# Attention queries made a batch ahead as rows of tokens, turned by VectorE and through DRAM

## The reference

```python
lat = layer_norm(latents, ln2_w, ln2_b)
lat = lat * (1.0 + scale[:, None, :]) + shift[:, None, :]
q = jnp.einsum('bld,ed->ble', lat, Wq)
kv_in = jnp.concatenate((x, lat), axis=-2)
kv = jnp.einsum('bld,ed->ble', kv_in, Wkv)
logits = jnp.einsum('bhqd,bhkd->bhqk', q * attn_scale, k * attn_scale)
w = jax.nn.softmax(logits.astype(jnp.float32), axis=-1).astype(logits.dtype)
out = jnp.einsum('bhqk,bhkd->bhqd', w, v)
return jnp.einsum('ble,de->bld', out, Wo)
```

## Time and profile before

| | |
|---|---|
| time, median of 3 runs | 685.08 us (683.45 to 686.34) |
| the profiled execution's own time | 684.31 us |
| its span, first to last instruction | 682.6 us |
| granted TensorE clock, mean | 0.997 |
| busy: TensorE, weight loads | 671.4 us (98%), 625.0 us (92%) |
| busy: VectorE, ScalarE, GpSimd | 470.2 us (69%), 430.6 us (63%), 269.2 us (39%) |
| query products, L1052 | 64.0 us in 512 passes |

### The profile page before, as it was taken

The page is one execution under the profiler, slowest core; times in us unless marked ns, Lnnn a source line. Parts: engine busy times, 40 slices in busy tenths (PEclk is TensorE's granted clock), DMA queues, the critical chain, the costliest instruction groups (busy, mean ns, idle before and its releaser), DMA issues. The chain is left out here.

```text
span 682.6 us, 17910 instructions
## 1 busy us (share of the span) xinstructions
PE 671.4 (98%) x5935; PEld 625.0 (92%) x5936; DVE 470.2 (69%) x970; ACT 430.6 (63%) x1166; POOL 269.2 (39%) x428
## 2 busy tenths in 40 slices
PE   8899999999999999999999999999999999999997
PEld 8789899999998999989989988898899999999997
DVE  7787877877787788787797766366645775444443
ACT  4888878788788888888878855242334554222222
POOL 2853243342433343324547441056520453424333
PEclk9899999999999999999999999999999999999999
DMA  7645455455455444545546434002668999888870
GB/s 279 190 121 149 121 145 146 130 146 146 124 140 150 131 131 138 156 120 139 147 132 171 106 94 132 1 1 96 180 217 244 299 346 294 256 266 258 259 245 5
DMA packets 77935, 111.76 MB, mean 164 GB/s; under 512 B 28732, under 2 KB 45758, under 8 KB 77632
## 3 DMA queue, kind: packets, MB, share of 16 engines
q1 hardware_dynamic: 66016, 92.73, 45.7%
q0 software_dynamic: 8864, 18.38, 9.5%
q10 hardware_dynamic: 3008, 0.03, 0.3%
HBM read 63.74 MB, written 16.67 MB: 118 GB/s over the span
## 5 line engine op out<-in xcount | busy, mean ns | idle before, releaser
L1034 PE MATMUL PS<-BIG 128*128 128x256 f32 (+1 forms) x1164 | 195.8, 322 | 3.1 <-ACT V L635 2.0
L1034 PEld LDWEIGHTS PS<-BIG 128*128 128x128 f32 x1164 | 163.9, 190 | 20.3 <-issue 5.1
L653 ACT ACTIVATE PR<-PS,NMX 128x256 f32<-128x256 f32 x256 | 119.2, 483 | 40.9 <-DVE NMX L838 40.9
L2092 PE MATMUL PS<-XST,W 128*128 128x128 f32 x1012 | 117.0, 275 | 0.3 <-DMA W<-in_w 0.3
L2092 PEld LDWEIGHTS PS<-XST,W 128*128 128x128 f32 x1012 | 115.1, 192 | 0.5 <-DMA W<-in_w 0.5
L496 POOL DMA_DIRECT2D PT<-PR x128 | 65.3, 515 | 125.0 <-DVE PR L850 81.0
L662 ACT ACTIVATE PR<-PR,RINV 128x256 f32<-128x256 f32 x256 | 106.1, 519 | 0.0
L850 DVE STREAM_TRANSPOSE PR<-PR 128x512 f32<-128x512 f32 x124 | 82.2, 691 | 4.6 <-ACT PR L662 1.5
L838 DVE TENSOR_REDUCE NMX<-PS 128x4 f32<-128x1024 f32 x64 | 75.6, 1201 | 0.1
L1587 POOL DMA_INDIRECT out_x<-YS,WHO x23 | 31.7, 1377 | 87.7 <-DVE YS L1954 76.9
L1052 PE MATMUL PS<-KVF,WQ 128*128 128x128 f32 x512 | 64.0, 278 | 0.0
(11 more groups left out here) (187 smaller groups left out, 1101.1 us busy)
## 6 DMA issues: line engine op xcount, KB each, us to landing
PT<-PR SPq DMA_DIRECT2D x368, 64.0 KB, 2.3
W<-in_w SPq DMA_DIRECT2D x29, 640.0 KB, 4.5
W<-in_w SPq DMA_DIRECT2D x21, 768.0 KB
PT<-PR POOLq DMA_DIRECT2D x128, 64.0 KB, 2.5
turned<-CXN SPq DMA_DIRECT2D x15, 256.0 KB, 2.0
INT<-turned POOLq DMA_DIRECT2D x56, 64.0 KB, 2.8
xs_sorted<-C SPq DMA_DIRECT2D x26, 128.5 KB, 3.0
W<-in_w SPq DMA_DIRECT2D x8, 352.0 KB, 3.4
```

Source lines behind the costliest of these rows:

```text
L653: last = act.activation(probs, logits, ACT.Exp, bias=NMX[:, g, own, p % 2:p % 2 + 1], accum_out=SUM[:, p, own:own + 1])
L1034: last = pe.matmul(dst, stat(s, k), mov(m, k), start=n == 0, stop=n == len(todo) - 1)
L2092: last = pe.matmul(h[:, P * c:P * (c + 1)], lhs13(W13[par], k, c), XST[par][:, :, k, :], start=k == 0, stop=k == KD - 1)
```

## The change

The queries of h = 6 to 29 (`TURNED`, batches 3 to 14) are made in another way and earlier.

- TensorE (`q_turned`): six products of 512 columns in the split form, tokens stationary, weights moving, so that bank 4 holds rows of tokens. Both halves of batch b+1 are made in batch b: the first half's behind the keys in the first half of b, the second half's where the next batch's first half stood. The rounded query weights WQS lie in the memory that WS13, the shared expert's weights, takes later; GpSimd splits them in batch 1 (`queries_split`).
- VectorE (`q_turn`) transposes the bank in 32x32 blocks into QT; SyncE (`store_queries`) stores it to DRAM; GpSimd (`load_queries`) loads it in four DMAs with the blocks exchanged, as QF. ScalarE (`q_hi_turned`) and VectorE (`q_lo_turned`, four subtractions of 128x128) make the high and low part from QF.
- Since keys and values of b+1 are now read in the first half of b, the inputs come earlier: from batch 1 on statistics, rows, conditions and input transpose of batch b+2 are in the first half of b and not in the second, and `modulate(b + 2)` is in the second half of b, where before `modulate(b + 1)` was in the first half of b. SyncE loads the rows of b+3 in batch b, GpSimd loads INT of b+2 at the end of batch b. ScalarE's KVH of the next batch goes from the end of the first half's normalisation to the start of the half.
- The descriptor memory of GpSimd's DMAs is halved, to make room for QT and QF.

The diff, cut to its core:

```diff
+            "queries": [dram(f"queries{i}", [P, INNER // 2]) for i in range(2)],
...
+TURNED = (6, 2 * NB - 3)
...
+    views["WQS"] = [w[:, :, :].rearrange("p k f -> p (k f)")[:, 0:KD * INNER].rearrange("p (h k e) -> p h k e", h=2, k=KD)
+                    for w in views["WS13"]]
...
+            def store_queries(h, H):
+                sp.wait_ge(v_qt, nth_turned(h))
+                sp.nop(nofuse=True)
+                sp.dma_start(mem["queries"][H], QT[:, :]).then_inc(d_qs, 16)
...
+            def batch(n, stored=True, rows=True, second=False, last=False, ahead=False):
+                if ahead:
+                    store_queries(2 * n + 2, 0)
+                if stored:
+                    store_inputs(n + 2)
                 if rows:
-                    load_rows(n + 2)
-                if first:
-                    load_inputs(sp, 1)
-                    load_late()
+                    load_rows(n + 3)
                 move_probs(n, 0)
-                if not first:
-                    load_residual(n - 1)
-                    if not second:
-                        store_sum(n - 2)
-                if rows:
-                    store_inputs(n + 2)
+                load_residual(n - 1)
+                if not second:
+                    store_sum(n - 2)
+                if ahead:
+                    store_queries(2 * n + 3, 1)
                 if not last:
...
+            def load_queries(h, H):
+
+                pool.wait_ge(d_qs, 16 * nth_turned(h))
+                pool.nop(nofuse=True)
+                pool.wait_ge(v_q, h)
+                pool.nop(nofuse=True)
+                for i in range(4):
+                    pool.dma_start(QF[QUADS[i], :, :],
+                                   mem["queries"][H][:, 128 * i:128 * (i + 1)].rearrange("(j c) f -> c j f", j=4))\
+                        .then_inc(d_qf, 16)
+
+            def queries_split(H, k):
+
+                parts = [t.rearrange("x (i p c) -> x i p c", i=4, p=HP) for t in (WQS[0][:, H, k, :], WQS[1][:, H, k, :])]
+                raw = WQ[:, H, k, :].rearrange("x (p i c) -> x i p c", i=4, p=HP)
+                pool.tensor_copy(parts[0], raw).then_inc(p_wqh, 1)
+                pool.wait_ge(p_wqh, KD * H + k + 1)
+                pool.tensor_tensor(parts[1], raw, parts[0].bitcast(FP32), ALU.subtract).then_inc(p_wql, 1)
+
+            def batch_1():
+                keep_probs(0, 1)
+                load_inputs(pool, 2)
+                kv_lo(2, 0)
+                norms(3)
+                keep_probs(1, 0)
+                load_inputs(pool, 3)
+                for H in range(2):
+                    for k in range(KD):
+                        queries_split(H, k)
+
+            def batch(b, par, following=True, norm=True, between=None, turned=True, ahead=True):
                 if following:
                     kv_lo(b + 1, 1 - par)
-                if not (isinstance(b, int) and b == 1):
-                    rstd(3, 1, v_mv3, p_ve3, p_rs3, b - 1)
+                if turned:
+                    load_queries(2 * b + 1, 1)
+                keep_probs(b - 1, 1)
+                if norm:
+                    norms(b + 2)
+                early_parts = HP if between else 0
+                for j in range(early_parts):
+                    between(j)
+                rstd(3, 1, v_mv3, p_ve3, p_rs3, b - 1)
+                if ahead:
+                    load_queries(2 * b + 2, 0)
                 keep_probs(b, 0)
                 if norm:
-                    norms(b + 2)
+                    load_inputs(pool, b + 2)
...
+            def q_hi_turned(h, H):
+                act.wait_ge(d_qf, 64 * nth_turned(h))
+                act.nop(nofuse=True)
+                act.wait_ge(t_lg, 2 * (h - 1))
+                act.activation(QH[:, HP * H:HP * (H + 1), :].rearrange("x p (j r) -> x j p r", j=4),
+                               QF[:, :, :].rearrange("x j (p r) -> x j p r", p=HP), ACT.Copy, scale=QSCALE).then_inc(a_q, 1)
...
+            def q_turn(h):
+                dve.wait_ge(t_q, h + 1)
+                if not (isinstance(h, int) and h == TURNED[0]):
+                    dve.nop(nofuse=True)
+                    dve.wait_ge(d_qs, 16 * (nth_turned(h) - 1))
+                dve.transpose(QT[:, :], PS[:, PROJ[0], :]).then_inc(v_qt, 1)
+
+            def q_lo_turned(h, H):
+                dve.wait_ge(a_q, h + 1)
+                for p in range(HP):
+                    low, high = (t[:, HP * H + p, :].rearrange("x (j r) -> x j r", j=4) for t in (QL, QH))
+                    last = dve.scalar_tensor_tensor(low, QF[:, :, 32 * p:32 * (p + 1)], QSCALE, high.bitcast(FP32),
+                                                    ALU.mult, ALU.subtract)
+                last.then_inc(v_q, 1)
...
-            def half_0(b, par, first=False, second=False, last=False):
+            def half_0(b, par, first=False, second=False, norm=True, turned=False, ahead=False):
                 h = 2 * b
                 row_max(h, 0)
-                q_lo(h + 1, 1)
+                if not turned:
+                    q_lo(h + 1, 1)
                 row_max(h, 1)
                 k_lo(h + 1, 1, 0)
                 k_lo(h + 1, 1, 1)
                 inverse_sums(h, 0)
-                if first:
+                if first or second:
                     modulate(b + 1, 1 - par)
+                if norm and not first:
+                    norm_stats(b + 2)
+                if ahead:
+                    q_turn(h + 2)
                 inverse_sums(h, 1)
+                if norm and not first:
+                    norm_rows(b + 2)
+                    conditions(b + 2)
+                    transpose_inputs(b + 2)
                 if not first and not second:
                     residual(b - 2)
-                transpose_blocks(h, 0, 0)
-                if not first and not last:
-                    modulate(b + 1, 1 - par)
-                for p in (1, 2, 3):
+                if turned:
+                    q_lo_turned(h + 1, 1)
+                for p in range(HP):
                     transpose_blocks(h, 0, p)
...
+                if ahead:
+                    q_lo_turned(h + 1, 0)
+                elif not final:
+                    q_lo(h + 1, 0)
                 if not final:
-                    q_lo(h + 1, 0)
                     for p in (0, 1):
                         transpose_blocks(h, 1, p)
                 else:
                     residual(b - 1)
-                if norm:
+                if first:
                     conditions(b + 2)
                     transpose_inputs(b + 2)
+                if norm and not first:
+                    modulate(b + 2, par)
+                if ahead:
+                    q_turn(h + 2)
                 if not final:
                     for p in (2, 3):
                         transpose_blocks(h, 1, p)
...
+            def q_turned(h, b, H, par):
+
+                if H == 0:
+                    pe.wait_ge(p_wql, 2 * KD)
+                    pe.wait_ge(a_kvh, b + 1)
+                    pe.wait_ge(p_kvl, b)
+                    if isinstance(h, int) and h == TURNED[0]:
+                        pe.wait_ge(v_q, h)
+                    else:
+                        pe.wait_ge(v_qt, nth_turned(h) - 1)
+                else:
+                    pe.wait_ge(v_ol, h - 3)
+                kv = (KVH[par], KVL[par])
+                split3(PS[:, PROJ[0], :], lambda s, c: kv[s][:, c, P:KEYS], lambda m, c: WQS[m][:, H, c, :],
+                       range(KD)).then_inc(t_q, 1)
...
+                    if taken is not None:
+                        pe.wait_ge(v_qt, nth_turned(taken))
...
-                if not first:
+                if not first and not turned:
                     q_unit(h + 1, b, 1, par)
                 for i in range(2):
                     k_unit(h + 1, b, 1, par, i)
+                if ahead:
+                    q_turned(h + 2, b + 1, 0, 1 - par)
...
-                    times_v(h - 2, b - 1, 1, 1 - par)
+                    times_v(h - 2, b - 1, 1, 1 - par, taken=h + 1 if ahead else h if turned else None)
                 if not final:
                     for i in range(2):
                         k_unit(h + 1, b + 1, 0, 1 - par, i)
-                    q_unit(h + 1, b + 1, 0, 1 - par)
+                    if ahead:
+                        q_turned(h + 2, b + 1, 1, 1 - par)
+                    else:
+                        q_unit(h + 1, b + 1, 0, 1 - par)
```

More of the change, by code:

```diff
@@ L439, in _ @@
             clear_rows(1)
-            with sp.Fori(2, NB - 2) as n:
-                batch(n)
+            with sp.Fori(2, NB - 3) as n:
+                batch(n, ahead=True)
                 clear_rows(n)
+            batch(NB - 3, rows=False, ahead=True)
+            clear_rows(NB - 3)
             sp.wait_ge(p_wsl, FT)
             load_w13(1)
-            batch(NB - 2, rows=False)
-            batch(NB - 1, rows=False, last=True)
+            batch(NB - 2, stored=False, rows=False)
```

(11 more changed lines are left out.)

117 lines of the change are left out of this document (66 added, 51 removed).

## The result

The changed kernel takes 729.54 us (median of four runs, 727.75 to 731.53) and the kernel before 684.72 us (683.45 to 686.34). The ratio is 1.0655, 95% interval 1.0635 to 1.0675: slower by 45 us. The forecast was 715, range 697 to 730.

A forecast was written before the change was run, and what follows sets the result against it. TensorE, without idle time, was taken to bound the kernel before; after the change VectorE's late subtraction would stall it. 684.3 us plus 24.5 for stalls and edges gave 709, plus 6 for the clock 715, range 697 to 730.

The forecast's parts named there:

- The removed work: TensorE's halves shrink to 12.5 and 11.6 us through shorter query units: 0.6 us a batch, 7 us in 12 batches.
- VectorE's start of the row maxima: On VectorE, the first half's row maxima start 3.0 us behind their logits, not 2.13.
- The first half: On VectorE, from the row maxima's start through the late query subtractions to TensorE's next logits: 10.9 us.
- the edges: Batches around the steady stretch: batch 1 +4.4, batch 2 +1.4, first stalled batch +2.4, batch 14 -0.8 us.
- The stall: TensorE waits some 2.3 us for VectorE's query subtraction at the second half's logits, eleven times, in batches 3 to 13.
- The clock: TensorE's granted clock falls after stalls, 1.6 us each time; four drops taken, +6 us, out of 0 to 17.6.
- Batch 1: VectorE waits 4 us there for the load of batch 3's rows: +4.4 us, 6 at most.
- At nothing, with its cover: Costs put at zero because hidden: the queries' DRAM round trip, extra stores and loads, earlier key and value parts, weight splitting.
- A: Rival: VectorE keeps up and TensorE stays the bound; 682 us, not slower; chance 0.07.
- B: Rival: the stall at the logits is near 1.2 us and the clock holds; 697 us; chance 0.10.
- C: Rival: GpSimd's queue of extra DMAs makes the power 2 us late, delaying normalised rows and subtraction; 731 us; chance 0.10.
- main case: The forecast itself, VectorE's late subtraction stalling TensorE's second-half logits: 703 to 728 us, chance 0.73.

The follow-up runs named there:

- e1_lo_early: The changed kernel with VectorE's four query subtractions moved from behind the residual to just behind the second reciprocal; 708.25 us, ratio 1.0358.
- e2_fill: The changed kernel with 16 extra, overwritten products of 256 columns on TensorE ahead of the second half's logits in batches 3 to 14; 716.54 us.
- e4_edge: The changed kernel with, in batch 1, VectorE's last reciprocals ahead of the statistics and GpSimd's power ahead of kv_lo; 727.02 us.
- e6_edge2: e4_edge with batch 3's rows also loaded ahead of SyncE's second probability moves of batch 0, and the reciprocals ahead of modulate; 724.17 us.
- e5_ring: e1_lo_early with two first-half block transposes put behind the next row maxima, and GpSimd's inputs load ahead of the kept moves; 708.3 us.
- e3_inputs: The changed kernel with only the inputs' new schedule kept and the queries made as before the change; 700.15 us, ratio 1.0237.
- e9_trip: e5_ring with the query transpose ahead of modulate, the store ahead of the last three probability moves, and the load ahead of kv_lo; 730.16 us.
- e11_store: e5_ring with only SyncE's store of the second query half put ahead of the last three probability moves; 714.86 us.
- e7_all: e1_lo_early, e5_ring and e6_edge2 joined, plus ScalarE copying the first tile of values ahead of its last normalisation; 703.52 us.

## Why the prediction held, point by point

- **The removed work.** 12.5 and 11.6 us a half were forecast. Where nothing waited they took 12.34, and 11.8 in e1_lo_early. The gain is real, some 0.5 us a batch.
- **VectorE's start of the row maxima.** Forecast 3.0 us behind the first half's logits; measured 3.12 (293.04 against 289.92).
- **The first half.** From there to the next logits 10.9 were forecast and 10.7 measured (303.74). The four subtractions took 0.90 us and put off what stood behind them by 0.81 (277.36 less 276.55). I had taken 1.03. The Trainium skill's fixed cost and rate ("VectorE: DVE Perf Modes", TRN2 errata) gave an estimate of 0.78; the trace lies between, nearer the rule when the next start counts. Two slips of the working are small: by its own terms (2.9, 0.92 and 0.60) the second key subtraction starts at 4.4, not 4.3, and the edges and stalls sum to 24.4, not 24.5.
- **The stall.** Forecast 2.3 us in eleven batches; measured 2.0 to 2.3 in nine of them, 4.21 in batch 3 and 3.44 in batch 13. In batch 3 the store of the queries took 4.4 us to land (2.7 is the median), GpSimd's loads waited for it, and VectorE's rows for the power behind the loads; GpSimd, then VectorE:

```profile
104.01 2.18 POOL L536 DMA_DIRECT2D QF<-queries  x4 [3.15 <-DMA queries<-QT]
```

```profile
109.22 0.41 DVE L859 TENSOR_SCALAR CXN<-RC,MV,RS 128x256 f32<-128x256 f32 x1 [2.41 <-POOL RS L504]
```

  In batch 13 small operations of VectorE were slower while GpSimd split late weights (last section). The eleven batches without the clock cost 19.9 us, against a forecast of 19.4. This is the step that carries the prediction, and e1_lo_early showed it: 21 us, the clock's share among them, go with the place of four instructions.
- **The clock, mis-sized.** I took four drops of 1.6, +6; there were nine, 14.0 us, and e2_fill gave back 13.0. The one row that I had spoke for a drop after every such stall, and the discount to four had no row behind it.
- **Batch 1, mis-sized.** +4.4 was forecast, with 6 as its upper bound; +11.3 came, and 0.9 in batch 0. The step that was too small is "VectorE would be at them at about 45; with the 3 us of a load it waits 4": the wait was costed on VectorE alone. What was queued behind the statistics, the reciprocals, was not followed round through ScalarE and GpSimd back to VectorE's own next input. e4_edge and e6_edge2 gave 3.4 and 5.8 us of it back by order alone, 2.6 and 4.9 with the half behind it (2.5 and 5.4 in the medians). The rest of the 11.3 is open.
- **At nothing, with its cover.** The round trip through DRAM was hidden in the changed kernel in every batch but one: ScalarE's copy of the second half's queries waits at most 0.4 us for the load. Batch 3 is the exception, with 2.75 us ahead of 108.77. The cover was the stall. With it gone (e5_ring) the trip ends last, 1.47 us late at 260.08. e3_inputs adds that the inputs' shift was not free in the steady state either: 0.45 a batch that the forecast had inside the stall.
- **Rivals.** A (VectorE keeps up, 682) fell: even e1_lo_early, with the subtraction early, is at 708. B (a short stall, clock held, 697) fell by both its terms. C (GpSimd's power late, 731) gives nearly the right time for the wrong reason: normalised rows (L859) waited 0.29 us for the power in the steady state, not 2. Its mechanism came once, in batch 3, with 2.41 us.
- **The number.** 715 against 729.5. The two mis-sized terms, 8.0 and 7.8 us (11.3 and batch 0's 0.9, less 4.4), make up the difference and a little more, and they lay on one side. The range held by half a us, and by luck: 729.5 lies above the main case's own 703 to 728, two of the four runs lie above 730, and the upper end, put between the main case and C, was right by its place and not by its reasons.

## What to carry to other kernels

An instruction that the bounding engine waits for is to be costed by its place in its own engine's queue, not by its length: four instructions of 0.2 us, once a batch, cost 21 us because they stood last. When a step is put ahead of others, follow each of those others round all engines until the loop closes, and do it again for every repair: kv_lo and the probabilities' buffer were each on such a loop, and e5_ring, e9_trip and e11_store gained nothing or lost because I followed only the loop that I wanted to shorten. A cost hidden in a stall comes back when the stall is mended.

## What the hardware showed that I had not expected

- Waits of TensorE of 2.0 to 2.3 us ahead of the second half's logits were followed by the 1.2 GHz level in seven of nine cases, and a wait of 3.44 us was not; its windows:

```profile
388.00:390.00 2.00, 1.56 (x24) 1.49 (x24) 2.00 (x4) 0.00 (x0) 0.98 (x3) 1.00 0.32 73
390.00:392.00 2.00, 2.00 (x40) 1.94 (x38) 2.00 (x4) 0.07 (x1) 1.74 (x4) 1.00 0.10 33
```

  In e9_trip, waits of 2.54 to 2.75 us ahead of the query products left seven of eleven first halves at 14.6 us, which is 12.0 and the wait, without a drop. What decides it these runs don't tell.
- Idle time costs more than itself: in the changed kernel 28.6 us of waits at the logits carried 14.0 us of lowered clock with them, and filling them with work that is thrown away made the kernel faster.
- Some small operations of VectorE took twice their time beside GpSimd's. In batch 13 of e7_all the four subtractions took 1.82 us, not 0.90, while GpSimd ran the split of late weights; VectorE, then GpSimd:

```profile
354.92 1.82 DVE L908 SCALAR_TENSOR_TENSOR BIG<-QF,BIG 128x128 fp32r<-128x128 f32 x4 [2.33 <-ACT BIG L692]
```

```profile
354.54 0.72 POOL L594 TENSOR_TENSOR BIG<-STAGE,BIG 128x256 fp32r<-128x256 f32 x1
355.21 0.45 POOL L592 CAST BIG<-STAGE 128x256 fp32r<-128x256 f32 x1
355.74 0.85 POOL L594 TENSOR_TENSOR BIG<-STAGE,BIG 128x256 fp32r<-128x256 f32 x1
```

  L908 is L906 of the changed kernel, where it took 1.76 us in the same batch (at 386.62), beside the same split; in batches 3 to 12 it took 0.90 each time. L908 reads two operands from SBUF. The Trainium skill ("GPSIMD Engine Reference", Specifications) says that GpSimd shares its SBUF interface with VectorE and contends with VectorE's instructions of two SBUF inputs; the trace agrees, with 1.82 against 0.90 us. L860, which reads one tensor of rows, took 0.90 us beside the split too (at 383.80), not 0.41. No run takes the split away, so the cause rests on these rows.
